# Four layers of attention and experts on one core: the last layer's rows go straight to the output by an indirect DMA, and two bursts of scatters are placed anew

## The reference

```python
skip = x
xn = _rms_norm(x, scale)
ids = jnp.argmin(_dist2(xn, centroids), axis=-1)
for e in range(8):
    h = jnp.einsum('bsd,dh->bsh', xn, up_w[e])
    a, g = jnp.split(h, 2, axis=-1)
    y = jnp.einsum('bsh,hd->bsd', a * jax.nn.silu(g), down_w[e])
    out = jnp.where((ids == e)[..., None], y, out)
return out + skip
```

## Time and profile before

| | |
|---|---|
| Time, median of 3 runs | 1431.2 us (1429.47 to 1433.84) |
| The profiled execution's own time | 1423.8 us |
| Its span, first to last instruction | 1421.9 us |
| Granted TensorE clock, mean | 0.86 |
| Busy: PE, DVE, ACT, POOL | 1123.1, 914.1, 769.9, 763.4 us |
| Chain that ended last | PE 49%, DVE 21%, issue 10%, POOL 9%, ACT 5% |

### The profile page before, as it was taken

The page is one execution under the profiler, slowest core; times in us unless marked ns, Lnnn a source line. Parts: engine busy times, 40 slices in busy tenths (PEclk is TensorE's granted clock), DMA queues, the critical chain, the costliest instruction groups (busy, mean ns, idle before and its releaser), DMA issues.

```text
span 1421.9 us, 31199 instructions
## 1 busy us (share of the span) xinstructions
PE 1123.1 (79%) x11651; PEld 896.5 (63%) x11651; DVE 914.1 (64%) x2229; ACT 769.9 (54%) x1651; POOL 763.4 (54%) x792
## 2 busy tenths in 40 slices
PE   5999876699976778772499599896789999877691
PEld 4777665698965556551288377675667777654461
DVE  7988842310249999952033588999879888855242
ACT  3777544465667677640022387774256877644230
POOL 4666482543416887477506667742355666462344
PEclk9999976899988686655699799997799999977896
DMA  9900011232342111002123200002000000001233
GB/s 329 301 17 2 2 35 49 82 101 68 103 136 60 39 42 47 1 29 71 48 67 92 66 17 19 22 2 89 1 1 2 2 2 2 2 31 43 82 86 110
DMA packets 98181, 81.75 MB, mean 57 GB/s; under 512 B 8560, under 2 KB 87536, under 8 KB 97904
## 3 DMA queue, kind: packets, MB, share of 16 engines
q1 hardware_dynamic: 87792, 58.76, 14.2%
q0 software_dynamic: 10240, 20.99, 4.9%
HBM read 45.24 MB, written 34.47 MB: 56 GB/s over the span
## 4 chain that ended last, share of the span: by engine, by line
PE 49%; DVE 21%; issue 10%; POOL 9%; ACT 5%; another core or an unknown queue 4%; DMA 1%; SPq 0%; POOLq 0%; ACTq 0%; DVEq 0%
PE bP L578 5%; PE b L683 4%; PE bS L659 4%; PE bS L569 4%; PE bP L672 3%; POOL uni L2425 3%; PE bP L966 2%; DVE rt L101 2%; POOL F_xbuf L2559 2%; PE bS L802 2%; POOL gb L2375 2%; PE bP L811 2%; PE b L822 2%; PE b L569 2%
## 5 line engine op out<-in xcount | busy, mean ns | idle before, releaser
L2425 POOL TENSOR_TENSOR uni<-uni,mx 128x1024 f32<-128x1024 f32 x96 | 182.7, 1904 | 154.1 <-DVE mx L1794 103.0
L2559 POOL DMA_INDIRECT F_xbuf<-XA,idxS x160 | 156.5, 978 | 106.0 <-issue 37.1
L659 PE MATMUL bS<-uni,Qx 64*64 64x256 f32 x1536 | 123.0, 442 | 45.9 <-ACT uni L1122 37.3
L2375 POOL DMA_INDIRECT gb<-F_ybuf,idxG x104 | 108.2, 1041 | 70.1 <-issue 33.7
L683 PE MATMUL b<-Vall,uni 128*64 128x18 f32 x3072 | 117.5, 220 | 21.8 <-ACT uni L1169 15.8
L683 PEld LDWEIGHTS b<-Vall,uni 128*64 128x64 f32 x3072 | 108.8, 149 | 33.7 <-ACT uni L1169 18.0
L672 PE MATMUL bP<-k_ident,uni 128*128 128x128 f32 x768 | 122.2, 311 | 4.4 <-ACT uni L1163 4.2
L1169 ACT ACTIVATE uni<-bP 128x512 f32<-128x512 f32 x192 | 106.2, 595 | 35.2 <-PE bP L672 29.8
L1163 ACT ACTIVATE uni<-uni 128x1024 f32<-128x1024 f32 x96 | 101.3, 1056 | 35.7 <-POOL uni L2425 35.3
L672 PEld LDWEIGHTS bP<-k_ident,uni 128*128 128x128 f32 x768 | 102.3, 162 | 18.6 <-issue 12.1
L659 PEld LDWEIGHTS bS<-uni,Qx 64*64 64x64 f32 x1536 | 55.4, 149 | 77.8 <-ACT uni L1122 42.6
(11 more groups left out here) (330 smaller groups left out, 2973.2 us busy)
## 6 DMA issues: line engine op xcount, KB each, us to landing
uni<-F_xbuf SPq DMA_DIRECT2D x28, 256.0 KB
F_ybuf<-uni SPq DMA_DIRECT2D x28, 256.0 KB
F_xbuf<-zero SPq DMA_DIRECT2D x1, 4992.0 KB, 16.9
uni<-ctx_dram SPq DMA_DIRECT2D x32, 128.0 KB
F_xbuf<-zero SPq DMA_DIRECT2D x1, 2944.0 KB, 12.8
F_xbuf<-zero SPq DMA_DIRECT2D x1, 2688.0 KB, 21.0
uni<-F_xbuf SPq DMA_DIRECT2D x16, 168.0 KB
F_ybuf<-uni SPq DMA_DIRECT2D x16, 168.0 KB
```

Source lines behind the costliest of these rows:

```text
L659: ins = T.matmul(o, pQx[v % 2][e][rows_, 128 * i + 64 * b:128 * i + 64 * b + 64], kx[rows_, :, tk], start=True, stop=True)
L2375: G.indirect_dma_start(gb[n], None, rows_, bass.IndirectOffsetOnAxis(ap=idxG[:, t, c:c + 1], axis=0)).then_inc(*gathered[n].up)
L2425: g.raises(G.tensor_tensor(s3, s3, mx3[t % 3][:, :].unsqueeze(2).to_broadcast([128, 16, 64]), ALU.subtract), b_sb, L, t)
L2559: G.indirect_dma_start(SP[L][0], bass.IndirectOffsetOnAxis(ap=idxS[:, t, c:c + 1], axis=0), XA[:, t, :], None).then_inc(*scat[c if L == "F ...
```

## The change

**The way back of F3.** `X` and `XA` (the normalised rows, which are what is scattered) become columns of one tensor `rows3` of 257 columns per tile: 128 of `XA`, 128 of `X`, and the token's number. F3's scatter writes all 257 columns (1028 bytes where there were 512). The fetched ring therefore holds, per row, the input, the row of `X` to be added, and where the row belongs. DVE adds the experts' result and the fetched `X` in one `tensor_tensor` where it copied before, and Pool scatters each finished chunk's 128 rows to `out` by the fetched token numbers: 46 indirect DMAs. Rows that hold no token carry the number 8192, beyond the output's 4096 rows, and are dropped by the bounds check. The stores to `F3_ybuf`, the 32 gathers, the 32 adds and the 8 plain writes of the output go. A ring buffer comes free at the group's `f_yo`, no longer when PE has turned it. `F3_xbuf` is zeroed with 257 columns a row.

**The order on Pool in F3.** After the first group's output scatters come the second half's 16 scatters, then the other output scatters.

**Epsilon.** `MV` in A0 and A1 keeps 1e-5 in a cell beside each variance and adds the two cells with a `tensor_reduce`; before, a `tensor_scalar` added the constant.

**The order on Pool at the ends of A0 and A3.** Tables `EARLY0` and `EARLY3` say at which step which scatters stand.

```diff
+        rows3 = sb("rows3", [128, NT, RW3])
+        XA, X = rows3[:, :, 0:128], rows3[:, :, 128:256]
+        token = rows3[:, :, 256].bitcast(mybir.dt.uint32)
...
         def sp_fetch(q, L, i, c, n):
-            q.wait_ge(f_et, L, i - 4)
+            q.wait_ge(f_yo if L == "F3" else f_et, L, i - 4)
...
             q.wait_ge(b_AV, "A3", NT - 1)
-            for g in range(3):
+            for g in range(NG3):
                 fetch(g)
-            for g in range(NG3):
...
-                sp_store(q, L, g, *GROUPS3[g])
-            for t in range(3, NT, 4):
-                q.wait_ge(f_cb, L, t)
-                q.e.dma_start(ov[:, t - 3:t + 1, :], X[:, t - 3:t + 1, :]).then_inc(*sent.up)
-            q.wait_ge(sent, L, 7)
+            for i in range(NO3):
+                q.wait_ge(sent[i], L, sum(n for _, n in GROUPS3[i::NO3]) - 1)
...
+        EARLY0 = {27: (0, 3), 28: (3, 6), 29: (6, 9), 30: (9, 12), 32: (12, 18), 34: (18, 21), 36: (21, 2 * HALF)}
+        EARLY3 = {29: (0, 5), 30: (5, 8), 31: (8, 10), 32: (10, 12), 33: (12, 14), 34: (14, 15), 35: (15, HALF3)}
...
             def MV(w):
-                V.tensor_scalar(m[:, 4:6], m[:, 1:4:2], 1e-5, None, ALU.add).then_inc(*t_ve.up)
+                V.tensor_reduce(mq[:, 6:8].unsqueeze(2), mq[:, 0:6].rearrange("p (i k) -> p i k", i=2)[:, :, 1:3], AX_X,
+                                ALU.add).then_inc(*t_ve.up)
...
         def dve_nearest(d, L, route):
-            def add(t):
-                d.wait_ge(gathered[t % 8], L, t // 8)
-                d.wait_ge(n_fx, L, t // 2)
-                V.tensor_tensor(X[:, t, :], X[:, t, :], gb[t % 8], ALU.add).then_inc(*f_cb.up)
...
+                    d.tick(V.tensor_copy(idxT[:, g, 0:n], ring[:, :, 256].bitcast(mybir.dt.uint32)))
                     d.wait_ge(f_dn, L, c)
-                    if g >= 2:
-                        d.wait_ge(stored[g % 2], L, g // 2 - 1)
-                    V.tensor_copy(uni[:, 9472 + 512 * (g % 2):][:, 0:n], YB[g % 2][:, 0:n]).then_inc(*f_yo.up)
+                    if g >= NO3:
+                        d.wait_ge(sent[g % NO3], L, GROUPS3[g - NO3][1] - 1)
+                    d.after(d.n)
+                    V.tensor_tensor(results3(g), YB[g % 2][:, 0:128 * n].rearrange("p (c d) -> p c d", c=n), ring[:, :, 128:256],
+                                    ALU.add).then_inc(*f_yo.up)
...
         def pool_nearest(g, L):
-            for t in range(HALF3, NT):
-                pool_scatter(g, L, t, 0, 1)
-            for h, groups in ((0, GA3), (1, NG3)):
...
+            to = out.rearrange("b s d -> (b s) d")
+            for i in range(NG3):
+                if i == 1:
+                    for t in range(HALF3, NT):
+                        pool_scatter(g, L, t, 0, 1)
+                g.wait_ge(f_yo, L, i)
+                for j in range(GROUPS3[i][1]):
+                    G.indirect_dma_start(to, bass.IndirectOffsetOnAxis(ap=idxT[:, i, j:j + 1], axis=0), results3(i)[:, j, :], None,
+                                         bounds_check=128 * NT - 1, oob_is_err=False).then_inc(*sent[i % NO3].up)
```

More of the change, by code:

```diff
@@ L30 @@
 HALF3 = 16
+RW3 = 257
 PARTS3 = ((0, HALF3), (HALF3, NT))
@@ L36 @@
 NG3 = len(GROUPS3)
+NO3 = 8
 GROUP3_OF = {c + j: g for g, (c, n) in enumerate(GROUPS3) for j in range(n)}
@@ L151, in build @@
         lnq = [sb(f"lnq{i}", [128, 8]) for i in range(4)]
+        fmq = [sb(f"fmq{i}", [128, 8]) for i in range(4)]
         lst = [sb(f"lst{i}", [128, 6]) for i in range(4)]
@@ L250, in build @@
         fetched = [sig(f"fetched{i}", 16, F0=NGF // 4, F1=4, F3=NG3 // 4) for i in range(4)]
-        stored = [sig(f"stored{i}", 16, F0=NGF // 2, F1=8, F3=NG3 // 2) for i in range(2)]
-        gathered = [sig(f"gathered{i}", 16, F0=8, F1=EARLY // 8 + (8 if i % 4 >= 2 else (NT - EARLY) // 4), F3=4) for i in range(8)]
+        stored = [sig(f"stored{i}", 16, F0=NGF // 2, F1=8) for i in range(2)]
+        gathered = [sig(f"gathered{i}", 16, F0=8, F1=EARLY // 8 + (8 if i % 4 >= 2 else (NT - EARLY) // 4),
+                       F3=sum(n for _, n in GROUPS3[i::NO3])) for i in range(NO3)]
+        sent = gathered
         f_c0 = sig("f_c0", F1=EARLY)
-        sent = sig("sent", 16, F3=8)
-        s_eo, s_exp, s_zero = sig("s_eo", su=1), sig("s_exp", su=1), sig("s_zero", su=1)
+        s_eo, s_exp, s_zero = sig("s_eo", su=1), sig("s_exp", su=1), sig("s_zero", su=2)
         s_tr, s_cc, s_bv, s_bo = sig("s_tr", su=8), sig("s_cc", su=8), sig("s_bv", su=1), sig("s_bo", su=1)
@@ L394, in sp_nearest @@
             q.wait_ge(b_AV, "A3", NT - 1)
-            for g in range(3):
+            for g in range(NG3):
                 fetch(g)
-            for g in range(NG3):
-                if g + 3 < GA3 or GA3 + 3 <= g + 3 < NG3:
-                    fetch(g + 3)
-                if g == GA3 - 2:
-                    for later in range(GA3, GA3 + 3):
-                        fetch(later)
-                sp_store(q, L, g, *GROUPS3[g])
-            for t in range(3, NT, 4):
-                q.wait_ge(f_cb, L, t)
-                q.e.dma_start(ov[:, t - 3:t + 1, :], X[:, t - 3:t + 1, :]).then_inc(*sent.up)
-            q.wait_ge(sent, L, 7)
+            for i in range(NO3):
+                q.wait_ge(sent[i], L, sum(n for _, n in GROUPS3[i::NO3]) - 1)
         def sp_program(e):
@@ L1004, in pe_nearest @@
         def pe_nearest(p, L):
-            xT3 = [uni[:, 6144 + 512 * i:6656 + 512 * i] for i in range(2)]
-            hm = [uni[:, 7936 + 256 * i:8192 + 256 * i] for i in range(3)]
-            hT = [uni[:, 8704 + 256 * i:8960 + 256 * i] for i in range(3)]
+            xT3 = [turned3(i) for i in range(2)]
+            _, hm, hT = zip(*(hidden3(i) for i in range(3)))
             HN = [b2p[:, :], bS[:, 0:512], bS[:, 512:1024]]
@@ L1356, in act_turn @@
             a.wait_ge(f_up, L, GROUPS3[i - 1][0] - 1 if i > 1 else -1)
-            S.activation(uni[:, 6144 + 512 * (i % 2):][:, 0:128 * n], b0[:, 0:128 * n], ACT.Copy).then_inc(*f_ec.up)
+            S.activation(turned3(i)[:, 0:128 * n], b0[:, 0:128 * n], ACT.Copy).then_inc(*f_ec.up)
         def act_sparse(a, L):
@@ L1428, in act_nearest @@
         def act_nearest(a, L):
-            gs = [uni[:, 7168 + 256 * i:7424 + 256 * i] for i in range(3)]
-            hT = [uni[:, 8704 + 256 * i:8960 + 256 * i] for i in range(3)]
+            gs, _, hT = zip(*(hidden3(i) for i in range(3)))
             HN = [b2p[:, :], bS[:, 0:512], bS[:, 512:1024]]
@@ L1515, in dve_setup @@
             d.tick(V.memset(rt[:, 1988:2116], 0.0))
+            for i in range(4):
+                d.tick(V.memset(fmq[i][:, 2:6:3], 1e-5))
             d.wait_ge(ld_small, "su", 0)
@@ L1550, in dve_masks @@
             d.tick(V.tensor_scalar(trash[:, :], K["DS"][:, 0:64], K["DG"], None, ALU.add))
+            d.tick(V.tensor_scalar(token, K["chunk"][:, 0:NT], 128.0, K["DG"], ALU.mult, ALU.add))
             for i in range(4):
@@ L2457, in pool_pairs @@
                     SB(s)
-                if kind == 0 and s >= HALF + 13:
-                    for t in range(2 * HALF):
-                        if t // 3 == s - HALF - 13:
-                            pool_scatter(g, "F0", t // 2, t % 2, 0)
+                if kind == 0 and s in EARLY0:
+                    for t in range(*EARLY0[s]):
+                        pool_scatter(g, "F0", t // 2, t % 2, 0)
                 if kind == 1 and s in EARLY1:
@@ L2549, in pool_cross @@
                     SL((s - 9) // 2)
-                if s >= HALF3 + 14:
-                    for t in range(HALF3):
-                        if t // 4 == s - HALF3 - 14:
-                            pool_scatter(g, "F3", t, 0, 0)
+                if s in EARLY3:
+                    for t in range(*EARLY3[s]):
+                        pool_scatter(g, "F3", t, 0, 0)
         def pool_scatter(g, L, t, c, h):
```

74 lines of the change are left out of this document (34 added, 40 removed).

## The result

The change takes 1425.3 us in the median of 20 runs (1414.4 to 1434.3), the kernel before 1430.5 beside it (20 runs, 1423.8 to 1436.4): a ratio of 0.9959, 95% interval 0.994 to 0.998. It is faster, by 5 us where 20 were forecast. The profiled execution has a span of 1419.9 us, 2.0 less than before. In a later session the ratio was 0.9990 (0.996 to 1.002), which is no difference.

What follows compares the result with a forecast made beforehand. Engines were thought nearly stopped while indirect DMAs run over about 6 us, with PE idle for F3's last 29.2 us. Terms -22 + 10 + 2 - 5 - 4 - 1 = -20 took the median from 1431.2 to 1411 us, range 1393 to 1433.

Steps and rivals of the forecast that it cites:

- Start and end of A0: A0: zeroing the larger F3_xbuf costs 0; powers moved ahead of scatters trim only Pool's pauses, -1 us (0 to -2).
- Epsilon: A1: the additions fall from 748 to 157 ns, 9.5 us of DVE's time, of which -5 us shows (0 to -9.5).
- End of A3: A3's end: two powers that began late behind scatters come earlier as five scatters move forward; -4 us (0 to -7).
- F3's first half: F3: Pool's burst grows from 16 to 24 indirect DMAs and the engines stand through the additional eight; +10 us (0 to +12).
- F3's second half: F3: two bursts of gathers are replaced by output scatters in bursts of four, 5.1 us each; +2 us (-3 to +10).
- The tail: F3's end: 29.2 us after the last group's copy shrink to 7.1, with three indirect DMAs, landing and SP's wait; -22 us.
- only the tail: Rival, chance 0.08: epsilon and the ends of A0 and A3 give nothing; 1421 us.
- The stall that does not grow: Rival, chance 0.20: F3's stop is a single event, Pool becomes the limit, span 37 us less, median 1394.
- instruction load: Within the non-growing stall rival: engines load 256 instructions at a time, so a stop from such a load comes only once.
- Output scatters: Rival, chance 0.12: bursts of four stop the engines in F3's second half, +30 us instead of +2; median 1439.

Runs made afterwards that it cites:

- a_held: The change with the second half's 16 scatters first and the first groups' output scatters held back until later groups are done; 0.9990 of the kernel before.
- p1: The change with the second half's 16 scatters first and one Pool memset before every further four scatters; 0.9875 and 0.9882 of the kernel before.
- a_mark: The change plus one Pool memset behind a wait for all output scatters, marking the last landing; profiled span 1442.5 us.
- a_first: The change with the second half's 16 scatters ahead of the first group's output scatters; 0.9944 of the kernel before.
- b_eps: The kernel before with the epsilon edit alone, in a session without stops; 1363.0 us against 1361.5, ratio 1.0013.

## Why the prediction was wrong

The profiles of the first pair, term by term (forecast, measured):

- **Start and end of A0**: -1, +3.4 (last scatter at 229.85 for 226.48). Of this 1.4 stood at the first subtraction on Pool (26.1 for 24.7), and that is no effect of the change: the same mark lies between 24.8 and 26.5 in all the other kernels, and at 26.2 in the kernel before run again. I had held one execution's start for fixed. The rest has the wrong sign: I counted what powers gain by coming forward and not that a power ahead of its input stops the scatters behind it. Over all runs that is 0.5 us. The zeroing of `F3_xbuf` took 35.1 us, 22 more where 13 were forecast, and that moved nothing: with 128 columns the first subtraction stands at 24.7 to 26.2, with 257 at 24.8 to 26.5.
- **Epsilon**: -5, 0. This is the first step that failed. I took 748 - 157 as work that disappears. It was a wait for a port that Pool held. The chain's 3.2% was such waiting too: in A1 of the kernel after (422 to 622), the chain has 6.0% on Pool's power (L2409), and DVE is busy 178.2 us where it was 180.1, not 9.5 less. From A1's first to its 32nd subtraction are 199.7 us before and 199.8 after.
- **End of A3**: -4, -5.3 here, -4.4 alone, -1.9 in the change again. Right, as far as single profiles tell.
- **F3's first half**: +10, +11.2. Right in cause and size, where there are stops: a_held, with a burst of 16, and p1, with lots of four, have 57.8 and 52.7 there, the kernel before 55.8 and 57.8. In a session without them the loss is nearly the same, 8.8 us, by another way: PE finishes early and stands 9.55 us for rows that were scattered 7 us later.
- **F3's second half**: +2, +3.3. Right.
- **The tail**: -22, -14.0 (29.8 to 15.8). This is the term that cost most. It had three scatters behind the last `f_yo`, and there were seven, because the two last groups' `f_yo` lie 1.1 us apart. Before they lay 1.55 us apart (1390.56 and 1392.11), so the trace of before had it: "Pool must be free by then" was written and tested on the mean interval of 7.3 us, not on the last one. From the end of the last `f_yo` (1404.65) to that of the last issue (1413.08) are 8.4 us where I had 3.8. The 3.3 for landing and SP's wait were 6.8; by a_mark 1.7 of them are the landing and the other 5.1 the end of the program, which I had put at 1. Together 8.1 us.

The sum is then +3.4 - 0.7 (F0) + 0.2 (A1) - 0.1 (F1 and A2) - 5.3 + 11.2 + 3.3 - 14.0 = -2.0, the difference of the spans. The medians are 5.2 apart: the profiled execution of the kernel before was the fastest of its 20, 6.7 us below their median, and that of the change lay 2.8 below its own.

Of the rivals, "only the tail" names the time nearest (1421), by luck: the other gains did appear at A3's end, and the tail was smaller. The stall that does not grow is refuted where there are stops. In sessions without them nothing held PE, as that rival had it, but the kernel before had no stops either, so the 37 us were not there to win. The stop is no instruction load either: in a_first, ACT stood 17.28 us up to 1354.31, and from 1331 to 1362 the profile's instruction queues carried nothing. Output scatters alone in bursts of four did not hold the engines; two groups that followed each other did a little (stops of 3.96 and 2.74 us on ACT at 1372.8 and 1384.1), three did more.

## What to carry to other kernels

Before an instruction is made shorter, see whether its duration is work: a small one that takes 1.2 us beside Pool and 0.16 elsewhere is waiting, and the wait moves on. Count the end of a program from the last instances themselves, with their own distances, not from a mean. Pool's indirect DMAs can be broken into lots of four by a short instruction of Pool's own where a burst stops the other engines, but measure in several sessions: the same pauses gave 2.6% in one kind of session and cost 1.2% in the other.

## What was not expected of the hardware

- The stops depend on something outside the program. With the first pair and in four later sessions the kernel before took 1430 to 1445 us with stops of 11 us on ACT; in two it took 1361 to 1363, with 52 indirect DMAs in a row in F1 and PE busy 35.7 of 36 us beside them. The chip's number does not decide it: number 2 and number 3 each had a session of either kind (whether a number is always the same chip is not on record). Of the 60.3 us between the spans of before and b_eps, 19.5 lie ahead of A1's first subtraction, 31.4 in F1 and A2 and 11.5 in F3's first half, stretches with long bursts of Pool in them; A3 takes 327.0 in both, and A1 is 3.4 shorter in before. What changes between the sessions stays open.
- In the sessions with stops, a burst of 16 or more stops PE, DVE and ACT until its end; lots of four with 1.15 us between them do not. Bursts of twelve end in stops of 6 to 7 us. Rows of 4 bytes stop them as rows of 1028 do. Whether the number of descriptors, their issue or something behind it is the cause, and whether an idle pause would do as well as a memset, was not tried.
- In the stopped stretch of F1 the granted clock of TensorE is 0.64 in the mean, between its two levels of 1.2 and 2.4 GHz, while PE is busy 8 of 36 us; with the pauses it is 0.92. Part of what the pauses give comes back by the clock.
- The span ends 7.0 us after the start of Pool's last instruction even if that is a memset of 0.15 us behind all landings.
